# Storing each pair's compressed tokens between its query stack and its key stack

## The reference

```python
w = xp.reshape(B, nW, WIN, H, hd)                      # windows of 128 tokens, 16 heads of 16
attn = softmax(einsum('bnqhd,bnkhd->bnhqk', w, w) * scale)
local = einsum('bnhqk,bnkhd->bnqhd', attn, w)
comp = conv1d(x, conv_w, stride 4) + conv_b            # 64 compressed tokens a row
gt = concatenate([comp, global_memory], axis=1)        # 128 global tokens
ga = softmax(einsum('bshd,bghd->bhsg', xm, gt) * scale)
glob = einsum('bhsg,bghd->bshd', ga, gt)
mix = sigmoid(concatenate([local, glob]) @ gate_w + gate_b)
out = (mix * local + (1 - mix) * glob) @ out_w + out_b
```

## Time and profile before

| | us |
|---|---|
| median of 3 timed runs | 1131.73 |
| lowest and highest of them | 1128.36, 1133.57 |
| the profiled execution | 1133.69 |
| its span, first to last instruction | 1131.9 |
| self-attention from pair 1's stack in use to its end | about 84 to 429 |

### The profile page before, as it was taken

One profiled execution on the slowest core, in us unless ns is written; L12 is line 12 of the kernel. 1 busy time (PEld: TensorE's weight loads), 2 busy tenths in 40 slices (PEclk: granted clock), 3 DMA queues, 4 the chain that ended last, 5 costly groups with the idle time before them and its releaser, 6 DMA issues.

```text
span 1131.9 us, 28588 instructions
## 1 busy us (share of the span) xinstructions
PE 1067.5 (94%) x11089; PEld 916.6 (81%) x11089; DVE 670.1 (59%) x1317; ACT 647.8 (57%) x872; POOL 554.5 (49%) x678
## 2 busy tenths in 40 slices
PE   7899999999999988999999997999999999999996
PEld 6777787777777766777777775898899999999995
DVE  4488888888888878788888886323324222222221
ACT  2366666665666665787777775444455444444441
POOL 5435355553445233433656665466754544444442
PEclk9899999999999999999999999999999999999999
DMA  8563634636355433665676557564432223332222
GB/s 215 150 180 98 184 107 125 166 94 169 110 137 139 123 96 72 173 170 165 150 165 176 145 159 250 142 138 51 43 54 48 48 48 48 52 52 48 48 43 24
DMA packets 174562, 130.22 MB, mean 115 GB/s; under 512 B 60810, under 2 KB 162927, under 8 KB 174432
## 3 DMA queue, kind: packets, MB, share of 16 engines
q1 hardware_dynamic: 155280, 106.79, 35.1%
q0 software_dynamic: 15840, 18.77, 11.6%
q10 hardware_dynamic: 3312, 2.85, 0.9%
HBM read 88.29 MB, written 40.08 MB: 113 GB/s over the span
## 4 chain that ended last, share of the span: by engine, by line
PE 51%; ACT 2%; issue 2%; another core or an unknown queue 2%; DMA 2%; POOL 1%; DVE 1%; POOLq 0%; ACTq 0%; SPq 0%
PE ps_scores L1990 22%; PE ps_out L2008 10%; PE ps_turn L1853 4%; PE ps_misc L1885 2%; PE ps_out L1865 2%; PE ps_misc L1806 2%; PE ps_scores L1840 2%; PE ps_misc L1873 1%; PE ps_turn L1969 1%; PE ps_scores L1833 1%; PE ps_scores L1914 1%; PE ps_misc L1879 1%; ACT weights L2181 1%; DMA weights<-q_scr 1%
## 5 line engine op out<-in xcount | busy, mean ns | idle before, releaser
L1990 PEld LDWEIGHTS ps_scores<-xgT,weights 128*128 128x128 f32 x2272 | 263.8, 192 | 9.2 <-ACT xgT L2205 3.4
L1990 PE MATMUL ps_scores<-xgT,weights 128*128 128x128 f32 x2272 | 266.1, 275 | 4.6 <-ACT xgT L2205 2.8
L2479 DVE TENSOR_TENSOR gate<-ps_scores,silu 128x512 f32<-128x512 f32 x71 | 49.1, 692 | 246.9 <-ACT silu L2221 222.7
L959 ACT ACTIVATE weights<-ps_scores 128x1024 f32<-128x1024 f32 x128 | 126.9, 1023 | 78.6 <-PE ps_scores L631 62.9
L2221 ACT ACTIVATE silu<-ps_scores 128x512 f32<-128x512 f32 x71 | 42.4, 597 | 210.6 <-PE ps_scores L1990 189.2
L2008 PE MATMUL ps_out<-w2s,gate 128*128 x560 | 132.6, 380 | 0.8 <-DVE y L2485 0.8
L2214 ACT COPY weights<-weights 128x2048 f32 x68 | 129.9, 1911 | 0.5 <-issue 0.3
L2008 PEld LDWEIGHTS ps_out<-w2s,gate 128*128 128x128 f32 x560 | 100.9, 190 | 12.0 <-issue 1.2
L1133 DVE TENSOR_REDUCE sa_rowmax<-ps_turn 128x8 bf16<-128x1024 f32 x64 | 77.8, 1215 | 36.7 <-PE ps_turn L608 36.7
L964 ACT CAST weights<-ps_scores 8x1024 bf16<-8x1024 f32 x64 | 64.3, 1005 | 56.0 <-PE ps_scores L622 56.0
L1676 POOL DMA_INDIRECT table<-entry,slot_i x64 | 65.0, 1016 | 38.8 <-issue 13.8
(11 more groups left out here) (325 smaller groups left out, 2115.4 us busy)
## 6 DMA issues: line engine op xcount, KB each, us to landing
weights<-w_scr SPq DMA_DIRECT2D x60, 256.0 KB, 3.9
weights<-q_scr SPq DMA_DIRECT2D x96, 128.0 KB
ks<-w_scr SPq DMA_DIRECT2D x24, 256.0 KB, 4.0
weights<-k_scr SPq DMA_DIRECT2D x48, 120.0 KB
w_scr<-wp SPq DMA_DIRECT2D x7, 768.0 KB, 3.8
q_scr<-qp SPq DMA_DIRECT2D x14, 384.0 KB
weights<-in_w1T SPq DMA_DIRECT2D x10, 512.0 KB
weights<-in_w3T SPq DMA_DIRECT2D x10, 512.0 KB
```

The source lines that it names most:

```text
L959: act.activation(probs[s % 2][:], m.scores[s % 2][:], ACT.Exp, scale=SCALE).then_inc(exped, 1)
L1990: mm = pe.matmul(h_ps[r % 2][:, j, c, :], weights[:, j, k, c * P:(c + 1) * P], xgT[r % 2][:, k, :], start=(k == 0), stop=(k == DT - 1))
```

## The change

SyncE's store_g(p) is called inside stack_w(p), after the six query loads and before the six key loads, and no longer after stack_w(p). It takes its waits with it. No other engine's instructions, no buffer and no size are altered.

```diff
@@ -296,6 +296,7 @@
             if p > 1:
                 sp.wait_ge(shifted, R * UPR * (p - 1))
             stack(qs[i].rearrange("k h r t -> k h (r t)"), w_scr[i], Q_PARTS, w_stacked, 64 * p, False)
+            store_g(p)
             stack(ks[i].rearrange("k h r t -> k h (r t)"), w_scr[i], K_PARTS, w_stacked, 64 * p + 32, True)
 
         def store_g(p):
@@ -374,7 +375,6 @@
             if p < NP - 1:
                 load_x(p + 1)
             stack_w(p)
-            store_g(p)
             store_keys_values(R * p - 1)
             load_ctx(R * p + 1)
             load_g(p)
```

## The result

The changed kernel takes 1164.11 us, the median of four runs (1160.70 to 1170.84), against 1130.05 us for the kernel before on the same chip: a ratio of 1.0285, 95% interval 1.0248 to 1.0322. It is 34 us slower. The profiled execution is the fastest of the four, 1160.70 us with a span of 1158.9, so its trace shows 27.0 us more than the trace of before. A second set of six runs gave 1163.6 us and a ratio of 1.0270 (1.0235 to 1.0305).

The account below looks back on a forecast made before the run. TensorE was taken to set the pace in self-attention. Stalls of 28.5 us, less 2 given back, plus 9 for the clock made 35.5 us on the 1131.73 us median: 1167 us, range 1147 to 1182.

Parts of the forecast that it names:

- The stop: SyncE's queue, pairs 1 to 7: the moved store waits 5.0 to 7.7 us for g_split, holding the key loads.
- From the split to line 608: Self-attention, pairs 1 to 7: six terms sum to 18.2 us after the split; PE waits 28.5 us in total.
- The term without a row: SyncE's key loads: the store just ahead holds them by 0.8 us, out of 0 to 1.5.
- In the shadow: Self-attention pairs: late keys and ScalarE's wait before overwriting kp, neither added to the sum unless its cover is gone.
- ScalarE on kp: ScalarE's line 950 stalls 2.5 us for the store of the cross keys before it overwrites kp.
- The clock: TensorE after its stalls: five of seven followed by slow clock at 1.8 us, 9 us, between 0 and 17.
- my upper bound: TensorE's clock in self-attention: falls after all seven stalls at 2.4 us each, 17 us.
- What the stall gives back: Self-attention: VectorE and ScalarE catch up during PE's stalls, 0.3 us a pair, 2 us.
- The stall without the clock: Self-attention, rival A: PE stalls but no clock loss, 26.5 us, 1158 us; chance 0.2.
- Only the keys late: Self-attention, rival B: gs lands quickly, keys and ScalarE's stall cost 13 us, 1144 us; chance 0.06.
- The hidden loads: Self-attention, rival C: the chain fits in the 14.1 us there are, nothing changes, 1132 us; chance 0.04.
- Faster than before: SyncE's queue, rival D: store lands under key loads, gs sooner, 0.9 us back at pair 1, 1131 us; chance 0.02.

Follow-up runs that it names:

- the wait alone: Kernel before with only the wait on g_split put between query and key loads, the store staying behind the keys: 1170.80 us, ratio 1.0344.
- the store without a stop: Kernel before with the store of g issued by GpSimd right behind the split, off SyncE's queue: 1130.60 us, ratio 0.9986.
- the filler: Changed kernel with nine identity matmuls on PE ahead of the wait on gs in pairs 1 to 7: 1156.97 us, then 1158.67 in a second run.
- the second trace: Changed kernel run once more, unaltered, beside the second run with nine filler matmuls: 1163.60 us.
- the cross stores moved: Changed kernel with the cross-attention key and value stores and context load put ahead of the store of g: 1141.65 us, ratio 1.0091.
- the keys last: Changed kernel with the key loads put behind the gs loads: 1198.25 us, ratio 1.0576.
- the fillers of 18: Changed kernel with 18 identity matmuls on PE ahead of the wait on gs in pairs 1 to 7: 1163.65 us, ratio 1.0289.

## Why the prediction was right, and where its sizes were off

I forecast 1167 us, 35.5 over the median before; measured were 1164.1, 34 over. Step by step:

- **The stop.** Forecast 5.0 to 7.7 us in each of seven pairs; measured 44.8 us in seven. Shown by the wait alone (+39 us) and by the store without a stop (no loss).
- **From the split to line 608, 18.2 us.** Measured 17.2 to 17.6. The terms: store to next issue 0.54, measured 0.4; keys with the store ahead 6.8 + 0.8 = 7.6, measured 7.1; the three issues 2.1, measured 1.7 to 2.8; gs from first issue to last landing 7.6, measured 6.8 to 7.8. The term without a row, the store ahead of the keys, was 0.8 out of 0 to 1.5; the comparison with the wait alone puts it at 0.65, and the base of 6.8, read from three query stacks, was 0.4 too high for keys. With 0.7 less in each of seven pairs the stall is 3.4 us a pair, not 4.1: 23.5 us in place of 28.5. The keys with the store ahead, 0.5 us too long, are most of it; this stall is the term of weight that was mis-sized.
- **In the shadow.** Keys about 1 us a pair: measured 6.1 in seven. ScalarE on kp: forecast 2.5 us, measured 1.7, with no wait of PE of its own behind it. Both lie within the 3.4.
- **The clock.** I took five falls at 1.8 us, 9 us. The first trace has six, after seven stalls, and they cost 6.7 us against the filler's trace at full clock: 5.3 in the six ways between stalls and 1.4 behind pair 7's. In the second trace it is 10.5: two of its falls last twice as long, and one more comes at 433 us, with no wait on gs ahead of it. So the number was about right, but not its make-up: a short fall costs 1.1 us and not 1.8. I had said that all work takes twice as long at half the clock; the windows show three quarters or seven tenths of the matmuls done, not half. The 2.4 us for each fall in my upper bound has no row; the long ones measured 2.2. The Trainium skill (TensorE: Matmul & The Clock Gate, "HAM oscillation") says that such waits on a DMA can send the clock down in every step, and the trace agrees: six in seven.
- **What the stall gives back.** I had counted 2 us. The six ways between stalls, where the clock is full, sum to 205.9 to 206.2 us in four traces (the cross stores moved, the keys last, the fillers of 18 and of the first 9) against 207.0 before: about 1 us, half of what I took.
- **The rivals.** The stall without the clock (1158) is nearly what the filler made, 1157 and 1158.7. Only the keys late (1144) is near what became of the kernel when the cross stores were moved, 1141.7, with 1.4 us a pair on the keys. The hidden loads didn't come: with other traffic about, a load of 256 KB landed after 3.9 us. The fit that I had cited for this rival, in the Trainium skill (DMA: Bandwidth & Descriptors, "Anatomy of one DMA"), is given there for DMAs that GpSimd issues, and these loads are issued by SyncE, so it doesn't bear on them. Faster than before needs g split before the last query load; even where the store's place cost nothing, the gain stayed within what can be told.

The mechanism was right: the stop, the late gs, the keys within its shadow, the falls of the clock. That the sum came so near, 35.5 against 34, is in part luck. At the end of self-attention the two traces of the changed kernel show 29.8 and 31.3 us more than the trace before: the stall 23.5 and 23.8, the clock 6.7 and 10.5, less 1 given back, and the first split 0.6 us later in one and 1.9 sooner in the other. For these executions my sum is 4 to 6 us too high, and the stall alone is too high by 5. The medians lie further apart than the first pair of traces: the profiled execution before took 3.6 us more than its median, that of the changed kernel 3.4 less. The clock may be a part of that. Of the ten timed runs of the changed kernel, the six under 1165 us had a mean granted clock of 0.980 to 0.984, the four above it of 0.975 to 0.977; I have no trace of one of those four.

## What to carry to other kernels

A store that is moved forward in an in-order queue carries its wait with it; ask not when its data are wanted but when they exist, and count the time of every issue behind it from that moment. The loss is the first need that this count misses, and it can be taken back by filling the stop with issues that are ready, by placing the store after its data exist, or by giving it to an engine that makes the data and so never waits. Where the waiting engine is TensorE, add a fall of its clock: here 12 of 14 waits of 2.4 to 3.2 us were followed by one, for 1.1 us each, or 2.2 where it lasted twice as long.

## What the runs showed that I had not expected

- The store of g, 288 KB, landed 4.2 us after its issue in the kernel before, with key loads in flight, and 2.8 us in the changed kernel, where it leaves after the stop with no loads ahead of it (medians of eight). The same DMA is slower by half behind other loads.
- The gs stack took 6.8 to 7.8 us from first issue to last landing behind the keys, and 3.2 to 4.1 us in the kernel with the keys last. A length read from one order of a queue doesn't hold in another.
- Pair 1's stall of 2.94 us had no fall of the clock behind it, while pair 3's of 2.37 us had. The length of the wait alone doesn't decide.
- A matmul of 128 x 128 in float32 is two instructions in the trace; eighteen took 4.24 us, 0.236 us each.
- Moving the store to GpSimd costs that engine 0.91 us an issue, which nothing waited for.
